# Early copies, weight sums moved to VectorE, and logits steps regrouped in a FFN kernel with LoRA and a two-expert layer

## The chip, the cores and the metric

The kernel runs on one core of one Trainium2 chip. The metric is the device time of one launch in microseconds (us), taken as the median of several runs; a profiled execution gives the trace. TensorE is written PE (PEld for its weight loads), VectorE DVE, ScalarE ACT, GpSimd POOL and SyncE, whose queue issues most DMAs, SP.

## The reference

There are 2048 tokens (8 sequences of 256) of width 1024. First a gated FFN with an adapter chosen for each sequence, then a layer in which each token takes the mean of two of eight experts, added to x:

```python
gate = x @ W_gate.T + (x @ A_gate[i].T) @ B_gate[i].T * 0.5
up   = x @ W_up.T   + (x @ A_up[i].T)   @ B_up[i].T   * 0.5
act  = silu(gate) * up                       # width 2752
y    = act @ W_down.T + (act @ A_down[i].T) @ B_down[i].T * 0.5
logits = y @ Wg + bg                         # 8 experts
top2 = top_k(logits, 2)
out = x + mean_k relu(y @ W_e[k] + b_e[k])   # k in top2
```

All inputs are float32.

## The kernel before

**Arithmetic.** Every fp32 operand is split into a high and a low half in a shorter format: ACT copies it (`w_hi`, `x_hi`, `a_hi`, `d_hi`), then DVE or POOL subtracts (`w_lo`, `x_lo`, `a_lo` on DVE; `d_lo` on POOL). A product is three matmuls (L1637 to L1639). The two large products are done by a seven-product scheme in place of eight: the operands are halves of matrices and their sums (B11, B21, T1 to T4, B22 for x; four sums of weights in the tiles `S_T` to `S_T+3`).

**Stages.** The tokens go in two groups g = 0, 1 of 1024. For each group, TensorE first does 21 pairs q of weight tiles with seven products j each (gate and up), with a half unit after them, then seven stages s of the down product, each of five pieces kp, with a remainder after stages 1, 4, 5 and 6. Piece and remainder together are numbered m = 0 to 38. Sums of weights are made by `mix_w` on POOL; for the first pair of the first group by `mix_w0` on DVE. After a product, `e_copy` (ACT, L1086) and `c_add` (DVE, L1115) take the results out of PSUM, so that the next product of the pair can be accumulated; product j = 3 needs copy k = 0, j = 4 copy 1, j = 5 copy 2 and the last part of j = 6 copy 3. `d_add` (DVE, L1209) takes the stages' results out, and a stage's fourth bank is free only when the first `d_add` of the stage before is done. The adapter of the down product needs `ad_diff`, `ad_hi`, `ad_lo` (L1001, L1007, L1012), which split a block that SP loads at L485; the first matmul of it (L1751) comes after the first piece of a group.

**Logits.** For the first half of a group's tokens DVE computes the logits: 64 calls of `l_step` (L1263) a group, each a multiply and sum over 512 columns with a row of the gate weights. SP loads these rows into two buffers of `ytp` (`load_wb`, L538); the load for row s waits until all four steps of row s - 2 are done. After step 63 come `l_sum` and `choice` (L1244, L1247). TensorE's `early_ranks` (L1898), which is placed behind the third piece of the last stage of g = 1, waits for that choice. For the other half TensorE turns y (`turn2`), ACT copies it (`lt_copy`) and TensorE multiplies (`sum2`, L1890); this is done between the last products of a group and the first ones of the next.

**Order of the work.** Each engine but TensorE has a list of jobs, each added with a key, written by hand in the time of TensorE's operations; the engine executes them in order of the keys, waiting at each for its semaphores:

```python
for _, _, fn, args in sorted(self.jobs, key=lambda j: j[:2]):
    fn(eng, *args)
```

`op(g, n)` is the time of product n (position `pos(q, j)`), `op_m(g, m)` = 228 g + 150 + 2 m that of piece m. A job that waits holds everything behind it on its engine, the DMAs of SP included. The keys around the change:

```python
act.add(key, a_hi, ...);  dve.add(key + 0.2, a_lo, ...)   # key = op_m(g, m) - 3.95
pool.add(op_m(g, m) - 3.5, d_lo, g, m)
sp.add(max(op_m(g, m) - 8.6, ...), load_a, j)             # pieces of the activation
```

Of the kernel before, what the change touches and what calls it, by code (L numbers as in the profile page):

```python
# [10 lines left out]
ALU = mybir.AluOpType  # L11
# [113 lines left out]
def build(nc, xp, xn, wp, agu, bgu, bdn, itok, wgt, wgb, bg, we, be, cst_f, cst_i, ident_d, ut_d, out):  # L125
# [6 lines left out]
    with ctx:  # L132
# [455 lines left out]
        for i in range(i, len(pieces)):  # L588
# [5 lines left out]
            sp.add(keys[i], load, i)  # L594
        for o, key in (("T2", op_m(0, 36) + 1.9), ("T3", op(1, 0) + 1.0), ("T4", op(1, 0) + 3.4)):
            for h in range(2):
                sp.add(key + 0.02 * h, load_x1, o, h)
# [25 lines left out]
        def l_key(g, o):  # L623

            if o < 32:
                return stage_end(g, 1) + 1.5 + 0.88 * o
            return stage_end(g, 4) + (0.3 + 0.45 * (o - 32) if g else 0.6 + 0.6 * (o - 32))

# [121 lines left out]
        for g in range(NG):  # L750
            for q in range(NP):
                if g or q:
                    pool.add(op(g, 0.5 if q == 1 else 7 * q - (6.5 if q else 4.6)), mix_w, g, q)
# [189 lines left out]

        def mix_w0(e, part):

            a = [[w_raw(0, i, j) for j in range(2)] for i in range(2)]
            if part == 0:
                arrived(e, at["w", 0, 0])
                arrived(e, at["w", 0, 1])
                e.tensor_tensor(tile(S_T), a[1][0], a[1][1], ALU.add).then_inc(s_S, 1)  # L950
                e.wait_ge(s_S, 1)
                e.tensor_tensor(tile(S_T + 1), tile(S_T), a[0][0], ALU.subtract).then_inc(s_S, 1)
            else:
                e.wait_ge(s_S, 2)
                e.tensor_tensor(tile(S_T + 2), a[0][1], tile(S_T + 1), ALU.subtract).then_inc(s_S, 1)
                e.tensor_tensor(tile(S_T + 3), a[1][0], a[0][0], ALU.subtract).then_inc(s_S, 1)
# [332 lines left out]
        for g in range(NG):  # L1289
# [12 lines left out]
            for o in XORD:  # L1302
                for h in range(2):
# [5 lines left out]
                    dve.add(key + 0.14, x_lo, g, o, h)  # L1309
            key = op(g, 0) + (0.05 if g else -1.745)  # L1310
            act.add(key, ag_hi, g)
            dve.add(key + 0.01, ag_lo, g)
            key = op(g, 150.95)
            dve.add(key, ad_diff, g)
# [23 lines left out]
            for q in range(NP):  # L1338
                for k in range(4):
                    key = 9.2 if q == 1 and k == 0 else pos(q, [0, 2, 3, 5][k]) + 1.05  # L1340
                    act.add(op(g, key), e_copy, g, q, k)
                    due = op(g, pos(q, [4 if q < 2 else 1, 6, 6, 6][k]) + [1.1, 1.05, 1.1, 1.15][k])
                    dve.add(due, c_add, g, q, k)
                    if q % 2 == 0 and (q < 20 or k < 2):
                        act.add(due + 0.35, silu, g, q, k)
                    if q % 2:
                        dve.add(due + 0.3, gated, g, q, k)
                    elif q == 20 and k >= 2:
                        dve.add(due + 0.3, gated, g, q, k - 2)
# [14 lines left out]
            for o in range(64):  # L1364
                dve.add(l_key(g, o), l_step, g, o)
            dve.add(l_key(g, 63) + 0.01, l_sum, g)
            dve.add(l_key(g, 63) + 0.02, choice, 2 * g)
            for m in range(8):
# [10 lines left out]
        for h in range(2):  # L1379
# [3 lines left out]
            dve.add(2.2 + 0.001 * h, x0_t4, h)  # L1383
        dve.add(-1.5, mix_w0, 0)
        dve.add(0.4, mix_w0, 1)
        for k in range(8):
# [247 lines left out]
        def _(e):  # L1634
# [50 lines left out]
            def product(g, q, j):  # L1685
# [5 lines left out]
                if j == 0:  # L1691
                    if q >= 2:
                        e.wait_ge(s_c, g * 85 + 4 * (q - 1))
                    elif g:
                        e.wait_ge(s_ev, 28 * g)
                    m = main1(g, n, "B11", bk, True, True)
                elif j == 1:
                    m = main1(g, n, "B21", bk + 1, True)
                    if q >= 2:
# [440 lines left out]
```

## Time and profile before

| | |
|---|---|
| median of 3 runs | 1919.98 us (1919.01 to 1924.09) |
| the profiled execution: its own time | 1930.36 us |
| its span, first to last instruction | 1928.2 us |
| mean granted TensorE clock | 0.979 of full speed |
| busy: PE, DVE, ACT, POOL | 96%, 63%, 39%, 56% |

The busy share is that of the whole span. A granted clock of 1.0 is the upper of the two levels (2.4 GHz), 0.5 the lower (1.2 GHz). Times in the trace count from the span's start. An idle time in a timeline row stands in brackets with what ended it.

### The profile page before, as it was taken

The numbers are of one execution on the slowest core, as the hardware profiler recorded it, in microseconds if no ns is written. First come the engines' busy times: TensorE is split into PE (matmuls) and PEld (weight loads), VectorE is DVE, ScalarE is ACT, GpSimd is POOL, SyncE is SP. The second block draws the span as 40 slices with busy tenths as digits, with TensorE's granted clock in tenths as the row PEclk, the third lists the DMA queues.
The fourth block names the chain that finished last, engine by engine and source line by source line (L and its number), as shares of the span: only waits on it lengthen the run. The fifth ranks groups of instructions, "written<-read, shape, count | busy, mean of one in ns | idle before, by whom it ended". The sixth has DMA issues, their size and how long they took to land.

```text
span 1928.2 us, 24887 instructions
## 1 busy us (share of the span) xinstructions
PE 1846.6 (96%) x8679; PEld 1540.2 (80%) x8679; DVE 1208.4 (63%) x1367; ACT 748.7 (39%) x1062; POOL 1084.0 (56%) x647
## 2 busy tenths in 40 slices
PE   4899999999899999999999998999989999999997
PEld 4788888888788878788888887887878888888886
DVE  8688778875458884776677766467886642344300
ACT  4444443443443333444444444343322333333332
POOL 3478888873334452464566643444433766666664
PEclk8999999999999999999999999999998999999998
DMA  5366665645466664344344345466633875677643
GB/s 195 103 219 221 223 222 194 234 154 171 165 228 232 214 197 137 107 130 155 121 150 169 132 140 181 164 232 211 206 116 131 238 190 138 180 188 189 156 90 55
DMA packets 118025, 331.43 MB, mean 172 GB/s; under 512 B 14080, under 2 KB 16000, under 8 KB 117632
## 3 DMA queue, kind: packets, MB, share of 16 engines
q1 hardware_dynamic: 99952, 268.06, 40.8%
q0 software_dynamic: 17952, 61.75, 13.4%
q8 instruction: 77, 1.26, 0.3%
q14 instruction: 44, 0.36, 0.1%
HBM read 248.62 MB, written 90.05 MB: 176 GB/s over the span
## 4 chain that ended last, share of the span: by engine, by line
PE 80%; DVE 7%; DMA 4%; issue 4%; POOL 2%; ACT 2%; SPq 1%; DVEq 0%; ACTq 0%; POOLq 0%
PE PS L1637 24%; PE PS L1638 24%; PE PS L1639 24%; PE PS L1681 2%; DVE FT L1263 2%; PE PS L1751 2%; PE PS L1983 2%; DMA raw<-wt_scratch 2%; DVE R L887 1%; PE PS L1890 1%; PE PS L1668 1%; DVE ring L868 1%; DMA X<-in_xp 1%; DMA FT<-act_scratch 1%; DVE R L918 1%
## 5 line engine op out<-in xcount | busy, mean ns | idle before, releaser
L1637 PE MATMUL PS<-R,ring 128*128 128x512 f32 (+1 forms) x1800 | 711.3, 395 | 41.2 <-issue 31.1
L1638 PE MATMUL PS<-R,ring 128*128 128x512 f32 (+1 forms) x1800 | 705.4, 392 | 0.0
L1639 PE MATMUL PS<-R,ring 128*128 128x512 f32 (+1 forms) x1800 | 704.4, 391 | 0.0
L1637 PEld LDWEIGHTS PS<-R,ring 128*128 128x128 f32 x1800 | 340.8, 189 | 114.3 <-issue 47.6
L1639 PEld LDWEIGHTS PS<-R,ring 128*128 128x128 f32 x1800 | 340.3, 189 | 72.5
L1638 PEld LDWEIGHTS PS<-R,ring 128*128 128x128 f32 x1800 | 340.9, 189 | 66.1
L748 POOL TENSOR_TENSOR ring<-raw,ring 128x1024 fp32r<-128x1024 f32 x78 | 193.2, 2477 | 294.6 <-ACT ring L874 294.5
L1637 PE MATMUL PS<-ring,R 128*128 128x512 f32 x592 | 235.5, 398 | 8.9 <-DVE FT L1209 8.9
L727 POOL DMA_INDIRECT brw<-in_bgu,idx_b x88 | 90.7, 1031 | 269.7 <-DVE R L1032 226.0
L868 DVE TENSOR_TENSOR ring<-FT,ring 128x512 fp32r<-128x512 f32 x168 | 178.6, 1073 | 91.0 <-ACT ring L864 89.3
L1638 PE MATMUL PS<-ring,R 128*128 128x512 f32 x592 | 234.0, 395 | 0.0
L1639 PE MATMUL PS<-ring,R 128*128 128x512 f32 x592 | 233.4, 394 | 0.0
L887 DVE TENSOR_TENSOR R<-FT,R 128x1024 fp32r<-128x1024 f32 x70 | 140.7, 2012 | 98.3 <-ACT R L883 97.9
L864 ACT ACTIVATE ring<-FT 128x512 fp32r<-128x512 f32 x168 | 105.8, 631 | 234.4 <-PE PS L1639 134.0
L1629 DVE CAST R<-raw 128x1024 fp32r<-128x1024 f32 x56 | 67.9, 1212 | 193.0 <-PE PS L1639 170.7
L874 ACT ACTIVATE ring<-raw 128x1024 fp32r<-128x1024 f32 x78 | 82.7, 1060 | 269.7 <-PE PS L1639 150.2
L868 DVE TENSOR_TENSOR ring<-raw,ring 128x512 fp32r<-128x512 f32 x130 | 152.4, 1174 | 53.7 <-ACT ring L864 51.1
L864 ACT ACTIVATE ring<-raw 128x512 fp32r<-128x512 f32 x130 | 81.2, 627 | 153.7 <-PE PS L1639 83.0
L1115 DVE TENSOR_TENSOR FT<-FT,PS 128x512 f32<-128x512 f32 x168 | 110.6, 679 | 47.4 <-PE PS L1681 47.3
L1637 PEld LDWEIGHTS PS<-ring,R 128*128 128x128 f32 x592 | 113.4, 192 | 33.3 <-DVE FT L1209 8.4
L1639 PEld LDWEIGHTS PS<-ring,R 128*128 128x128 f32 x592 | 113.0, 191 | 24.4
L1263 DVE CUSTOM_DVE_ANT_0 FT<-FT,ytp 128x512 f32<-128x512 f32 x128 | 125.5, 1023 | 8.8 <-DMA ytp<-in_wgb 8.7
(189 smaller groups left out, 2356.3 us busy)
## 6 DMA issues: line engine op xcount, KB each, us to landing
raw<-in_wp SPq DMA_DIRECT2D x124, 512.0 KB, 4.2
act_scratch<-FT SPq DMA_DIRECT2D x140, 256.0 KB, 4.8
FT<-act_scratch SPq DMA_DIRECT2D x70, 512.0 KB, 4.8
raw<-in_we SPq DMA_DIRECT2D x64, 512.0 KB, 6.3
raw<-wt_scratch SPq DMA_DIRECT2D x40, 512.0 KB, 6.2
out<-in_xn SPq DMA_DIRECT2D x17, 512.0 KB, 5.1
ytp<-in_wgb SPq DMA_DIRECT2D x32, 256.0 KB, 4.9
y_scratch<-FT SPq DMA_DIRECT2D x7, 1024.0 KB, 7.3
```

What stands on the lines that cost most here:

```text
L727: e.indirect_dma_start(out=brw[0:96, j * 512:(j + 1) * 512], out_offset=None, in_=bgu.rearrange("(r a) n -> r (a n)", a=2), in_offset=ioa( ...
L748: e.tensor_tensor(slot2(n, 1), pair(raw_t(i)), slot2(n, 0), ALU.subtract).then_inc(s_lp, 1)
L864: e.activation(slot(op(g, n), 0), w_src(g, n), ACT.Copy).then_inc(s_hi, 1)
L868: e.tensor_tensor(slot(op(g, n), 1), w_src(g, n), slot(op(g, n), 0), ALU.subtract).then_inc(s_lo, 1)
L874: e.activation(slot2(n, 0), pair(raw_t(i)), ACT.Copy).then_inc(s_hi, 2)
L887: e.tensor_tensor(a_ring(j, 1), raw_a(j), a_ring(j, 0), ALU.subtract).then_inc(s_al, 1)
L1115: e.tensor_tensor(c_tile(q, k), tile(E_T + [0, 2, 0, 1][k]), PS[:, bk + [1, 2, 3, 0][k], :], ALU.add).then_inc(s_c, 1)
L1263: e.tensor_tensor_reduce(out=JK[n % 2], in0=tile(SET_C + tt), in1=ytp[:, (s % 2) * 512:(s % 2) * 512 + 512], scale=1.0, scalar=0.0, op0=AL ...
L1629: link(e.tensor_copy(s_w_t(ex, k, 0), raw_t(i)))
L1637: e.matmul(out_, hi, whi, start=start, stop=False, skip_group_check=True)
L1638: e.matmul(out_, hi, wlo, start=False, stop=False, skip_group_check=True)
L1639: return e.matmul(out_, lo, whi, start=False, stop=stop, skip_group_check=True)
```

## The change

- The copies k = 0, 1, 2 of the first pair of the first group get keys 0.0, 0.25 and 1.25 in place of 1.05, 5.05 and 6.05, so ACT does them before the splits of the operands that come later.
- The four weight sums of the second pair of the first group are made by DVE (`mix_w0` with q = 1, keys 2.5 to 2.52) and no longer by POOL (key 0.5). The first pair's third and fourth sums are parted: keys 0.16 and 1.16 in place of 0.4 for both.
- The 64 logits steps of a group get keys op_m(m) + 2.3, which is 0.05 behind the `a_lo` of piece m + 3: two behind each piece in the first half (m = 10 to 25), then 2, 4, 4, 4, 4, 4, 3, 4, 3 (m = 26 to 34). `l_sum` and `choice` come at op_m(34) + 2.38. Before, the steps lay every 0.88 (first half) and every 0.6 (g = 0) or 0.45 (g = 1). SP's `load_wb` keys follow from the same function.
- The adapter's `ad_diff`, `ad_hi`, `ad_lo` of the down product move from op(g, 150.95) to op(g, 149.0).
- In the first products of g = 1: `ag_hi`, `ag_lo` move from 0.05 to 0.2, behind the split of T2 on ACT; the load of T4 from 3.4 to 2.9; the first product waits for the third `lt_copy` (and the second one for the fourth) in place of all `d_add`s of group 0.

```diff
--- before.py
+++ after.py
@@ -592,7 +592,7 @@
             if e >= 2 and k == 3:
                 sp.add(keys[i], load_bias, e)
             sp.add(keys[i], load, i)
-        for o, key in (("T2", op_m(0, 36) + 1.9), ("T3", op(1, 0) + 1.0), ("T4", op(1, 0) + 3.4)):
+        for o, key in (("T2", op_m(0, 36) + 1.9), ("T3", op(1, 0) + 1.0), ("T4", op(1, 0) + 2.9)):
             for h in range(2):
                 sp.add(key + 0.02 * h, load_x1, o, h)
         for j in range(70):
@@ -623,8 +623,10 @@
         def l_key(g, o):
 
             if o < 32:
-                return stage_end(g, 1) + 1.5 + 0.88 * o
-            return stage_end(g, 4) + (0.3 + 0.45 * (o - 32) if g else 0.6 + 0.6 * (o - 32))
+                m = 10 + o // 2
+            else:
+                m = 26 + sum(o - 32 >= n for n in (2, 6, 10, 14, 18, 22, 25, 29))
+            return op_m(g, m) + 2.3 + 0.001 * o
 
         for g in range(NG):
             for s in range(16):
@@ -749,7 +751,7 @@
 
         for g in range(NG):
             for q in range(NP):
-                if g or q:
+                if g or q >= 2:
                     pool.add(op(g, 0.5 if q == 1 else 7 * q - (6.5 if q else 4.6)), mix_w, g, q)
             for p in range(10):
                 pool.add(op(g, 14 * p) + 16.9, mix_act, g, p)
@@ -941,18 +943,25 @@
             e.wait_ge(s_xl, x_at(0, "B21", h))
             e.tensor_tensor(X0[2][:, hs], X0[2][:, hs], X0[0][:, hs], ALU.subtract).then_inc(s_xp, 1)
 
-        def mix_w0(e, part):
-
-            a = [[w_raw(0, i, j) for j in range(2)] for i in range(2)]
+        def mix_w0(e, q, part):
+
+            a = [[w_raw(0, 2 * q + i, j) for j in range(2)] for i in range(2)]
             if part == 0:
-                arrived(e, at["w", 0, 0])
-                arrived(e, at["w", 0, 1])
+                arrived(e, at["w", 0, 2 * q])
+                arrived(e, at["w", 0, 2 * q + 1])
+                if q:
+                    e.wait_ge(s_lo, lo_of(0, pos(0, 3)))
                 e.tensor_tensor(tile(S_T), a[1][0], a[1][1], ALU.add).then_inc(s_S, 1)
-                e.wait_ge(s_S, 1)
+                e.wait_ge(s_S, 4 * q + 1)
                 e.tensor_tensor(tile(S_T + 1), tile(S_T), a[0][0], ALU.subtract).then_inc(s_S, 1)
-            else:
-                e.wait_ge(s_S, 2)
+            elif part == 1:
+                e.wait_ge(s_S, 4 * q + 2)
+                if q:
+                    e.wait_ge(s_lo, lo_of(0, pos(0, 4)))
                 e.tensor_tensor(tile(S_T + 2), a[0][1], tile(S_T + 1), ALU.subtract).then_inc(s_S, 1)
+            else:
+                if q:
+                    e.wait_ge(s_lo, lo_of(0, pos(0, 5)))
                 e.tensor_tensor(tile(S_T + 3), a[1][0], a[0][0], ALU.subtract).then_inc(s_S, 1)
 
         def e_hi(e, k):
@@ -1307,10 +1316,10 @@
                         key = {"B11": -4.95, "B21": -3.95, "T1": -1.6, "T2": -0.7, "B22": 0.2, "T3": 1.3, "T4": 2.3}[o] + 0.02 * h
                     act.add(key, x_hi, g, o, h)
                     dve.add(key + 0.14, x_lo, g, o, h)
-            key = op(g, 0) + (0.05 if g else -1.745)
+            key = op(g, 0) + (0.2 if g else -1.745)
             act.add(key, ag_hi, g)
             dve.add(key + 0.01, ag_lo, g)
-            key = op(g, 150.95)
+            key = op(g, 149.0)
             dve.add(key, ad_diff, g)
             act.add(key + 0.01, ad_hi, g)
             dve.add(key + 0.02, ad_lo, g)
@@ -1338,6 +1347,8 @@
             for q in range(NP):
                 for k in range(4):
                     key = 9.2 if q == 1 and k == 0 else pos(q, [0, 2, 3, 5][k]) + 1.05
+                    if g == 0 and q == 0 and k < 3:
+                        key = [0.0, 0.25, 1.25][k]
                     act.add(op(g, key), e_copy, g, q, k)
                     due = op(g, pos(q, [4 if q < 2 else 1, 6, 6, 6][k]) + [1.1, 1.05, 1.1, 1.15][k])
                     dve.add(due, c_add, g, q, k)
@@ -1363,8 +1374,8 @@
                     dve.add(key, d_add, g, s, i)
             for o in range(64):
                 dve.add(l_key(g, o), l_step, g, o)
-            dve.add(l_key(g, 63) + 0.01, l_sum, g)
-            dve.add(l_key(g, 63) + 0.02, choice, 2 * g)
+            dve.add(op_m(g, 34) + 2.38, l_sum, g)
+            dve.add(op_m(g, 34) + 2.39, choice, 2 * g)
             for m in range(8):
                 key = [-1.5, -1.3, -1.0, -0.7, 0.3, 0.4, 0.5, 0.6][m] if g else [-1.5, -1.3, -1.0, -0.7, 1.0, 1.1, 2.0, 2.1][m]
                 act.add(stage_end(g, 6) + key, lt_copy, g, m)
@@ -1381,8 +1392,9 @@
             dve.add(-0.8 + 0.001 * h, x0_t2, h)
             dve.add(1.2 + 0.001 * h, x0_t3, h)
             dve.add(2.2 + 0.001 * h, x0_t4, h)
-        dve.add(-1.5, mix_w0, 0)
-        dve.add(0.4, mix_w0, 1)
+        for q in range(2):
+            for part in range(3):
+                dve.add([[-1.5, 0.16, 1.16], [2.5, 2.51, 2.52]][q][part], mix_w0, q, part)
         for k in range(8):
             act.add(keys[at["e", 0, k]], e_hi, k)
             dve.add(keys[at["e", 0, k]] + 0.1, e_lo, k)
@@ -1692,9 +1704,14 @@
                     if q >= 2:
                         e.wait_ge(s_c, g * 85 + 4 * (q - 1))
                     elif g:
-                        e.wait_ge(s_ev, 28 * g)
+                        if q:
+                            e.wait_ge(s_ev, 28 * g)
+                        else:
+                            e.wait_ge(s_lc, 8 * g - 5)
                     m = main1(g, n, "B11", bk, True, True)
                 elif j == 1:
+                    if g and q == 0:
+                        e.wait_ge(s_lc, 8 * g - 4)
                     m = main1(g, n, "B21", bk + 1, True)
                     if q >= 2:
                         m = lora1_out(g, q, 0, 0, bk + 1)
```

## Rows read from the trace of the kernel before

**Rows 1.** The first line of the page.

```profile
span 1928.2 us, 24887 instructions
```

**Rows 2.** Waits of TensorE (line, releaser: us in total, times, longest).

```profile
PE PS L1751 <- DVE R L1012: 11.7, 2, 5.8
...
PE PS L1898 <- DVE msk L1247: 3.9, 1, 3.9
```

**Rows 3.** Timeline of TensorE where it resumes: start, us, operation, [idle before <-releaser].

```profile
54.57 0.76 PE L1637 MATMUL PS<-R,ring 128*128 128x512 f32 x1 [16.28 <-issue]
...
493.59 1.22 PE L1751 MATMUL PS<-R 128*128 128x256 f32 x4 [5.84 <-DVE R L1012]
...
722.05 0.47 PE L1637 MATMUL PS<-ring,R 128*128 128x512 f32 x1 [2.12 <-DVE FT L1209]
...
737.00 0.77 PE L1637 MATMUL PS<-R,ring 128*128 128x512 f32 x1 [3.27 <-issue]
...
771.81 0.47 PE L1637 MATMUL PS<-R,ring 128*128 128x512 f32 x1 [1.36 <-issue]
...
777.38 0.47 PE L1637 MATMUL PS<-R,ring 128*128 128x512 f32 x1 [2.36 <-issue]
```

**Rows 4.** Windows: us, busy by engine, then PEclk, DMA share, GB/s.

```profile
493.50:498.50 5.00, 4.91 (x17) 4.24 (x18) 0.72 (x2) 2.00 (x2) 1.58 (x1) 0.55 0.00 0
722.00:727.00 5.00, 4.95 (x19) 4.13 (x20) 2.90 (x5) 0.60 (x1) 0.44 (x1) 0.66 0.62 223
...
1205.40:1211.90 6.50, 6.48 (x20) 5.52 (x21) 2.24 (x1) 2.00 (x2) 2.37 (x1) 0.54 0.01 3
```

**Rows 5.** Timeline of ScalarE, start-up.

```profile
53.87 0.60 ACT L1086 ACTIVATE FT<-PS 128x512 f32<-128x512 f32 x1
```

**Rows 6.** Timeline of VectorE, start-up.

```profile
29.51 2.35 DVE L918 TENSOR_TENSOR R<-FT,R 128x1024 fp32r<-128x1024 f32 x2
...
37.70 5.15 DVE L936 TENSOR_TENSOR X<-X,FT 128x1024 f32<-128x1024 f32 x2
42.78 3.43 DVE L918 TENSOR_TENSOR R<-X,R 128x1024 fp32r<-128x1024 f32 x2
...
52.42 0.68 DVE L868 TENSOR_TENSOR ring<-raw,ring 128x512 fp32r<-128x512 f32 x1
...
71.10 1.29 DVE L1115 TENSOR_TENSOR FT<-FT,PS 128x512 f32<-128x512 f32 x2 [0.56 <-PE PS L1681]
```

**Rows 7.** Timeline of GpSimd, start-up.

```profile
39.70 2.07 POOL L665 TENSOR_TENSOR FT<-FT,raw 128x512 f32<-128x512 f32 x1
```

**Rows 8.** Source view of the load of the adapter block, L485.

```profile
L485 SPq DMA_DIRECT2D FT<-ad_scratch x2: 319/319/319, 470.7 to 1183.5; - x2
...
DMA to landing us min/median/max: 3.9/3.9/4.0
```

**Rows 9.** Timeline of VectorE before the first stage.

```profile
478.12 2.48 DVE L1173 TENSOR_TENSOR R<-FT,R 128x512 fp32r<-128x512 f32 x1 [0.78 <-ACT R L1165]
...
490.58 0.56 DVE L1001 TENSOR_TENSOR FT<-FT 128x160 f32<-128x160 f32 x2
491.70 1.83 DVE L1012 TENSOR_TENSOR R<-FT,R 128x352 fp32r<-128x352 f32 x4 [0.56 <-ACT R L1007]
```

**Rows 10.** Source view of the logits step, L1263.

```profile
L1263 DVE CUSTOM_DVE_ANT_0 FT<-FT,ytp x128: 676/681/3226, 568.8 to 1428.9; 128x512 f32<-128x512 f32 x128
```

**Rows 11.** Source view of the low halves of the activation pieces, L887.

```profile
L887 DVE TENSOR_TENSOR R<-FT,R x70: 1211/2570/3420, 469.0 to 1433.2; 128x1024 fp32r<-128x1024 f32 x70
```

**Rows 12.** Timeline of VectorE, last stage of the second group.

```profile
1412.97 3.23 DVE L1263 CUSTOM_DVE_ANT_0 FT<-FT,ytp 128x512 f32<-128x512 f32 x1
...
1431.17 1.90 DVE L1244 TENSOR_TENSOR oh<-cf,mi 128x64 bf16<-128x64 f32 x1
```

**Rows 13.** Timeline of GpSimd, same stretch.

```profile
1413.23 2.41 POOL L748 TENSOR_TENSOR ring<-raw,ring 128x1024 fp32r<-128x1024 f32 x1
```

**Rows 14.** Timeline of ScalarE, fifth stage of the second group.

```profile
1335.26 1.06 ACT L874 ACTIVATE ring<-raw 128x1024 fp32r<-128x1024 f32 x1 [9.57 <-DMA raw<-in_wp]
```

More of the change, by code:

```diff
@@ L942, in x0_t4 @@
             e.tensor_tensor(X0[2][:, hs], X0[2][:, hs], X0[0][:, hs], ALU.subtract).then_inc(s_xp, 1)
-        def mix_w0(e, part):
-            a = [[w_raw(0, i, j) for j in range(2)] for i in range(2)]
+        def mix_w0(e, q, part):
+            a = [[w_raw(0, 2 * q + i, j) for j in range(2)] for i in range(2)]
             if part == 0:
-                arrived(e, at["w", 0, 0])
-                arrived(e, at["w", 0, 1])
+                arrived(e, at["w", 0, 2 * q])
+                arrived(e, at["w", 0, 2 * q + 1])
+                if q:
+                    e.wait_ge(s_lo, lo_of(0, pos(0, 3)))
                 e.tensor_tensor(tile(S_T), a[1][0], a[1][1], ALU.add).then_inc(s_S, 1)
-                e.wait_ge(s_S, 1)
+                e.wait_ge(s_S, 4 * q + 1)
                 e.tensor_tensor(tile(S_T + 1), tile(S_T), a[0][0], ALU.subtract).then_inc(s_S, 1)
-            else:
-                e.wait_ge(s_S, 2)
-                e.tensor_tensor(tile(S_T + 2), a[0][1], tile(S_T + 1), ALU.subtract).then_inc(s_S, 1)
+            elif part == 1:
+                e.wait_ge(s_S, 4 * q + 2)
+                if q:
+                    e.wait_ge(s_lo, lo_of(0, pos(0, 4)))
+                e.tensor_tensor(tile(S_T + 2), a[0][1], tile(S_T + 1), ALU.subtract).then_inc(s_S, 1)
+            else:
+                if q:
+                    e.wait_ge(s_lo, lo_of(0, pos(0, 5)))
                 e.tensor_tensor(tile(S_T + 3), a[1][0], a[0][0], ALU.subtract).then_inc(s_S, 1)
```

## The prediction

> **What bounds the kernel now.** The page first: a span of 1928.2 us [rows 1] of which TensorE is busy 96% (the table above), so what can be won is TensorE's idle time and its slow time. I read the waits of TensorE next, then its timeline at each idle place, and then, at each place, the queue of the engine that ended the wait. The waits view [rows 2] shows two waits of 5.84 us for the adapter's low halves (one a group) and one of 3.94 us for the first choice of the second group. The timeline [rows 3] shows the rest that the change touches: 16.28 us at 54.57 in the start-up, 2.12 us at the end of group 0, then 3.27, 1.36 and 2.36 us in the first products of group 1. After such an idle time TensorE also runs at the lower clock level: in the windows view [rows 4] the granted clock is 0.55 and 0.54 (near the 1.2 GHz level) after the two waits of 5.84 us, which loses 4.9 x 0.45 = 2.2 and 6.5 x 0.46 = 3.0 us, and 0.66 after the 2.12 us, which loses 1.7 us; the stretches after 737.00 and 777.38 look the same, 1.7 us each. After 1.36 us alone nothing is lost. All engines but TensorE have idle time, so an edit counts only by the wait that it ends. All terms are against the profiled execution (1928.2 us span, 1930.4 us with what lies around it); the runs shown have a median of 1919.98 us, 0.5% less, so I take the same microseconds off that.
>
> **Start-up.** TensorE resumes at 54.57 because product j = 4 waits for copy 1, which ACT executes at 53.87 [rows 3, 5]. The copy's source was complete at about 29 us (TensorE's timeline); it stood behind the splits of T3, T4 and of five weight tiles. With the new keys copies 0 and 1 run at about 28 and 31 us, and j = 4 is bound by the split of its weights on DVE. From here on DVE's queue sets the pace, so I count its work up to the split for j = 6, which ends at 53.1 [rows 6].
> - Removed: the sums of T3 and T4 and the low halves of T3 take 5.15, 3.43 and, at 46.73, 3.43 us again for two instructions of 128x1024 each, where such a pair takes 2.35 us undisturbed [rows 6]; GpSimd's weight sums run beside them (2.07 us each, [rows 7]). With those gone from POOL: -2.80 - 1.08 - 1.08 = -5.0 us.
> - Removed: about 1.1 us in which DVE waited for ACT at 33 us.
> - Added: four weight sums of 128x512 on DVE, each the size of the split at 52.42, 0.68 us less 0.07 of overlap: +2.5 us. They precede the split for j = 6 and delay it.
> - So that split ends near 49.5. Behind it are nine short instructions (two of the adapter's, three splits, one addition, two low halves of the adapter product, in all 5 us), which the adapter's part of j = 6 needs: 54.5, then copy 3 and four small matmuls: 55.2. In the trace the additions that follow j = 6 start at 71.10 [rows 6]. The difference is 15.8 us; I take 15.0, as a low-clock stretch may remain after the two shorter idle times (near 3.5 and 2 us). Bounds: 10 (copies help, the sums fill the rest) and 16.5.
> GpSimd's sums for the third pair start at once on the load that waits for the split of j = 6, so they move along.
>
> A rule of the Trainium skill speaks against the second half of this: Perfetto Trace Analysis, section Optimizing Scalar/DVE Operations, says that GpSimd and VectorE share a read port, so that moving work between them might not help. With it alone, the start-up would give about 12.5 in place of 15.0; the pairs of 5.15 against 2.35 us in [rows 6] rather show that the sum on DVE costs less than what it disturbs from POOL.
>
> **The adapter of the down product.** SP issues the block's load at 470.7 and it lands after 4.0 us [rows 8], at 474.7. DVE executes `ad_diff` at 490.58, last of its list before the stage, and `ad_lo` at 491.70, ended 493.5 [rows 9]. With the key 149.0 it comes behind the split at 478.12, which ends at 480.6: 0.56 + 0.56 of waiting for ACT + 1.83 = 483.6. TensorE needs it at 487.75, so the wait goes, with 4 us to spare. What is late instead: ACT holds the third piece's copies 1.5 to 3.5 us, `a_lo(2)` ends near 485.3 and POOL's low half near 487.4, needed at 495; the half unit's chain ends 2 us later, needed after 510. No wait arises. Both groups: 2 x 5.84 + 2.2 + 3.0 = 16.9 us. Bounds: 12 (the clock falls anyway) and 17.
>
> **Group 1's first products.** The first product writes bank 0; the third `lt_copy` has already been waited for by the matmul before it, so 3.27 us go. T4's load moves ahead of two weight loads of which the first waits for POOL; ACT reaches T4 early and copies 1 and 2, which stood behind it, follow their products: 1.36 + 2.36 us go. With the clock: 7.0 + 2 x 1.7 = 10.4 us. What could rise is `s_L` 5, needed by the second adapter product, with a margin of some 1.4 us. Bounds: 5 and 10.5.
>
> **Logits steps.** A step takes 0.68 us, 3.2 at most [rows 10], when GpSimd works beside it; 128 steps remain 128 steps. A piece's `a_lo` takes 1.21 to 3.42 us in the same way [rows 11].
> - End of group 0: five steps stood behind the last `a_lo`, now three. 2 x 0.61 us earlier, and the choice then runs before GpSimd's sums begin (1.8 us less); `d_add` of the last stage, now at 721.2, comes near 718.5, before TensorE's 719.93. -2.12 - 1.7 = -3.8 us. But in the fifth stage four steps, not three, precede the `d_add` of group 0, and the fourth meets GpSimd's next piece, as in group 1 at 1412.97 [rows 12, 13], where TensorE idled 0.9 us: +1.0 us. Net -2.8.
> - End of group 1: the choice that `early_ranks` waits for ends at 1433.3 [rows 12]. Before the last `a_lo` there were 63 steps, after the change 61; but the last `a_lo` and three steps come before the choice, and 54 to 58 are behind the `d_add` of stage 5. From there DVE has no idle time: five steps more (5 x 0.61) and one `a_lo` more (1.14 undisturbed): +4.2 us on a wait of 3.94, and a longer low clock as after 5.84 us, +0.9: +5.1 us. Bounds: +1 (GpSimd meets fewer of them) and +8.
> - First halves: steps 8 and 9, 18 and 19 still stand before the `d_add`s, so the waits there (1.21, 1.76, 2.89 us) stay. SP's `load_wb` waits for a step that comes 0.6 to 2.9 us later at two places: +1.0 us. Bounds: -2 and +5.
>
> Here one rule can be weighed. The trace has a step that starts at 1412.97, 0.26 us before GpSimd's instruction, and still takes 3.23 us [rows 12, 13]. The Trainium skill, SBUF — State Buffer, section Who interferes with whom, has it that whoever is first holds the shared pair of ports for the whole instruction and the other is blocked. By it the fourth step would take 0.68 us and the +1.0 would be 0; the row decides, and I keep it.
>
> **The sum.** -15.0 - 16.9 - 10.4 - 2.8 + 5.1 + 1.0 = -39.0 us. The profiled span would be 1889 us, the median 1919.98 - 39 = 1881 us. Behind the stages, in the expert blocks, nothing is changed, and TensorE is busy there, so all of it passes to the end.
>
> **Rivals.**
> - *The adapter's wait is taken up next* (13%): with TensorE 8 us ahead, the pieces' loads are late. For it: loads were issued during the 5.84 us. Against: the next three pieces' weights had landed by 490. It would give back half of 16.9: 1889.5 us.
> - *The load queue* (17%): in the first halves, `load_wb` stands directly in front of the activation and weight loads and waits for the two steps before it. For it: before 1335.26 ACT waited 9.57 us for a weight load [rows 14] that SP issued late behind such a `load_wb`, and TensorE then idled 2.89 us and lost 3.1 us by the clock, 6.0 in all. Two more such places: 1881 + 12 = 1893 us.
> - *Slower* (3%): the same queue at many places. It decides from seven more such places on (7 x 6.0 = 42 > 39); at eight, 1929 us. Against: SP waits for the same splits now as before, only 1 to 3 us longer.
> - *The change does not do what it says in the start-up* (5%): the sums on DVE cost what they free; 12.5 in place of 15.0: 1883.5 us. This is what the sharing rule above would give.
> - My forecast, 1881 us: 62%.
>
> **How the numbers follow.** The likeliest case with its own bounds reaches from 1872 to 1890; the queue's case with one more place goes to 1899, and I leave its tail and the slower case out: 1871 to 1899. A measurement of this kernel tells about 0.3% (6 us) from no change. Faster by more than that: 62 + 13 + 17 + 5 = 97%, less 2 for a queue case that eats nearly all: 95%. Same 2%, slower 3%.
>
> **What would show it.** Right: TensorE idle between 28 and 56 us is about 8 us, not 21; DVE's sums of T3 and T4 take 1.2 us each; no idle at the first L1751 of either group and a clock of 1.0 there; no idle at the first product of group 1; `early_ranks` waits about 8 us. Wrong: L1637 idle behind DMAs of SP in the second to fourth stage, more than 6 us in sum than before; `early_ranks` waiting 4 us or less (then I overrated the regrouping's cost, and the time is near 1876); or a new wait of the second adapter product for `s_L`.

## The result, and the profile after

The changed kernel takes 1906.02 us (median of 5 runs, 1903.87 to 1909.91), the kernel before, timed beside it, 1921.42 us (1919.01 to 1925.28). The ratio is 0.9923, 95% interval 0.9903 to 0.9942: 0.8% faster, 15 us. I had forecast 1881 us and a range of 1871 to 1899, so the direction was right and the size was not: less than half of the 39 us came. The profiled executions differ by 24.0 us (1904.2 against 1928.2 us span); 9 us more than the medians, since the one profiled execution of before was 9 us above its median. That part is looked at with the first experiment, e0.

The waits of TensorE in the changed kernel (line, releaser: us in total, times, longest):

```profile
PE PS L1649 <- DVE FT L1218: 17.3, 6, 6.6
PE PS L1649 <- DVE R L920: 9.4, 1, 9.4
PE PS L1915 <- DVE msk L1256: 8.7, 1, 8.7
PE PS L1649 <- DVE ring L870: 6.5, 3, 3.8
PE PS L1768 <- DVE R L889: 5.8, 2, 3.5
```

The 11.7 us of [rows 2] for the adapter's low halves are gone. `early_ranks` (now L1915) waits 8.7 us in place of 3.9. The first line had 8.9 us, 5 times, 2.9 at most before: TensorE now waits 17.3 us for `d_add` (L1218). The last line is new: TensorE waits for a piece's `a_lo` (L889). The timeline of TensorE shows the places:

```profile
34.60 0.50 PE L1649 MATMUL PS<-R,ring 128*128 128x512 f32 x1 [1.90 <-DVE ring L870]
49.86 0.50 PE L1649 MATMUL PS<-R,ring 128*128 128x512 f32 x1 [3.81 <-DVE ring L870]
55.34 1.02 PE L1693 MATMUL PS<-R 96*128 96x256 f32 x6 [1.02 <-DVE R L1063]
...
594.71 0.98 PE L1768 MATMUL PS<-R 128*128 128x256 f32 x6 [2.33 <-DVE R L889]
...
612.03 0.80 PE L1649 MATMUL PS<-ring,R 128*128 128x512 f32 x1 [6.55 <-DVE FT L1218]
...
712.53 0.47 PE L1649 MATMUL PS<-ring,R 128*128 128x512 f32 x1 [2.24 <-DVE FT L1218]
...
1302.58 1.21 PE L1768 MATMUL PS<-R 128*128 128x256 f32 x8 [3.47 <-DVE R L889]
...
1320.75 0.79 PE L1649 MATMUL PS<-ring,R 128*128 128x512 f32 x1 [5.79 <-DVE FT L1218]
...
1415.78 0.19 PE L1915 MATMUL PS<-msk,ut 128*128 128x12 bf16 x1 [8.70 <-DVE msk L1256]
```

The start-up (54.57 in [rows 3] is now 34.60) and the first products of group 1 (no idle time left there) went as forecast. The waits at 594 and 1302 stand at the last piece of stage s = 3, those at 612 and 1320 at the first piece of s = 4 (stages counted from 0), all in the first half of the logits steps. The windows view gives the clock beside them (columns as in [rows 4]):

```profile
474.00:479.00 5.00, 5.00 (x27) 4.31 (x26) 2.24 (x4) 3.98 (x6) 0.43 (x1) 1.00 0.34 108
...
612.00:620.00 8.00, 7.97 (x23) 6.38 (x24) 6.29 (x9) 3.06 (x3) 5.43 (x3) 0.64 0.81 269
```

At the adapter (474) the clock is now 1.00, where [rows 4] had 0.55; after the 6.55 us wait it is 0.64 for 8 us, 2.9 us lost.

**The same points of the program in both traces (milestones).** Both traces have 8679 matmul records in the same order, so the end of the same one is taken in both. The table gives what each stretch added to the changed kernel's lead, in us; a stretch is closed where TensorE is back at the full clock in both.

| stretch | forecast | profiled |
|---|---|---|
| start-up | -15.0 | -13.7 |
| adapter, both groups | -16.9 | -8.1 - 8.8 |
| first products of group 1 | -10.4 | -10.9 |
| first halves of the steps | +1.0 | +11.0 + 6.9 |
| end of group 0 | -2.8 | +1.3 |
| end of group 1 (`early_ranks` and the low clock after it) | +5.1 | +5.0 |
| what follows in group 1 (TensorE turning y, first experts) to the last product | 0 | -6.7 |

(The texts of e1 and e3 below carry a first reading with other bounds: 10.7 and 8.1 for the first halves, 1.9 for the end of group 0.) The first three terms hold within 1.3 us each. One term is off by 17 us, and it decided the outcome. For it, read what SyncE's queue does in stage s = 3 of group 0 (L538 is `load_wb`, L429 `load_a`, L412 and L416 loads of weights or of an operand):

```profile
582.30 0.33 SPq L538 DMA_DIRECT2D ytp<-in_wgb  x1
582.67 0.43 SPq L429 DMA_DIRECT2D FT<-act_scratch  x1
583.20 0.38 SPq L416 DMA_DIRECT2D raw<-wt_scratch  x1
583.62 0.43 SPq L416 DMA_DIRECT2D raw<-in_xp  x1
584.57 0.32 SPq L429 DMA_DIRECT2D FT<-act_scratch  x1
584.93 0.67 SPq L412 DMA_DIRECT2D raw<-in_wp  x1
598.11 0.33 SPq L538 DMA_DIRECT2D ytp<-in_wgb  x1
```

Six DMAs leave within 3.3 us, then none for 12.5 us, until the next `load_wb` goes. What happens in between, on ScalarE and then on VectorE:

```profile
590.07 1.06 ACT L876 ACTIVATE ring<-raw 128x1024 fp32r<-128x1024 f32 x1 [10.05 <-DMA raw<-wt_scratch]
591.03 1.04 ACT L885 ACTIVATE R<-FT 128x1024 fp32r<-128x1024 f32 x1
```

```profile
592.10 2.56 DVE L889 TENSOR_TENSOR R<-FT,R 128x1024 fp32r<-128x1024 f32 x1 [6.34 <-ACT R L885]
594.58 0.68 DVE L1272 CUSTOM_DVE_ANT_0 FT<-FT,ytp 128x512 f32<-128x512 f32 x1
...
595.19 2.88 DVE L1272 CUSTOM_DVE_ANT_0 FT<-FT,ytp 128x512 f32<-128x512 f32 x1
```

It is a closed loop through SyncE's queue, a load, ScalarE and VectorE. The weight tile issued at 583.20 lands at 590.0, ScalarE splits it (`d_hi`) and then the activation piece, `a_lo` follows, then the two steps 14 and 15, and at 598.07 the next `load_wb`, which waits for step 15, lets the next weight tile go. One turn takes 15.8 us (550.62, 566.40, 582.30, 598.11 are the issues of `load_wb`) and brings two pieces. TensorE needs 12.8 us for two. So each turn takes 3.0 us from the lead that the split pieces have over TensorE, and when the lead is used up TensorE waits: 2.33 + 6.55 us.

### The profile page after: what moved, and what is told of

It is laid out like the page before. It is cut to its first block, busy times and chain, and to the rows that moved or that the text cites. A ratio compares the mean times of both kernels' runs of the same rounds, so it can differ in the third digit from the quotient of the medians.

```text
span 1904.2 us, 24886 instructions
## 1 busy us (share of the span) xinstructions
PE 1835.0 (96%) x8679; PEld 1529.2 (80%) x8679; DVE 1205.3 (63%) x1371; ACT 748.5 (39%) x1062; POOL 1082.8 (57%) x643
## 4 chain that ended last, share of the span: by engine, by line
PE 72%; POOL 8%; DVE 8%; issue 5%; DMA 5%; ACT 1%; SPq 1%; POOLq 0%; ACTq 0%; DVEq 0%
PE PS L1649 22%; PE PS L1650 21%; PE PS L1651 21%; DVE R L889 2%; DVE FT L1272 2%; DMA raw<-wt_scratch 2%; PE PS L1693 2%; PE PS L2000 2%; PE PS L1768 2%; DMA raw<-in_wp 1%; POOL brw L729 1%; POOL FT L672 1%; POOL FT L667 1%; POOL FT L664 1%; PE PS L1907 1%
## 5 line engine op out<-in xcount | busy, mean ns | idle before, releaser
L1649 PE MATMUL PS<-ring,R 128*128 128x512 f32 x592 | 235.7, 398 | 17.7 <-DVE FT L1218 17.3
L889 DVE TENSOR_TENSOR R<-FT,R 128x1024 fp32r<-128x1024 f32 x70 | 148.4, 2122 | 117.8 <-ACT R L885 117.5
L1649 PEld LDWEIGHTS PS<-ring,R 128*128 128x128 f32 x592 | 113.4, 192 | 43.3 <-DVE FT L1218 17.6
L1651 PEld LDWEIGHTS PS<-ring,R 128*128 128x128 f32 x592 | 113.1, 191 | 24.3
L1650 PEld LDWEIGHTS PS<-ring,R 128*128 128x128 f32 x592 | 113.2, 191 | 22.0
```

The source lines that it names most:

```text
L889: e.tensor_tensor(a_ring(j, 1), raw_a(j), a_ring(j, 0), ALU.subtract).then_inc(s_al, 1)
L1649: e.matmul(out_, hi, whi, start=start, stop=False, skip_group_check=True)
L1650: e.matmul(out_, hi, wlo, start=False, stop=False, skip_group_check=True)
L1651: return e.matmul(out_, lo, whi, start=False, stop=stop, skip_group_check=True)
```

## The experiments

One thousandth of the time is 1.9 us; every ratio is to the kernel before, timed on the same chip, with its 95% interval.

**e0: the kernel before, a second profile.**

> The kernel before, once more, unchanged, for a second profile of it. The first profiled execution was 9 us above the median of its runs (1930.4 against 1921.4). If that was its clock alone, this one shows the same idle places (16.3 us at 54.6, 5.8 us twice, 3.3 and 2.4 us) and fewer low-clock stretches, above all in the one of 13.65 us near 1457 and of 12.66 us at the end. If the idle places differ, the waits themselves vary from run to run.

It took 1923.95 us (span 1921.9), with the same idle places within 0.5 us each, but for the 1.36 us at 771.81 [rows 3], which is 0.32 us in it. Of the 6 us between the two profiles nearly all lies behind 1300, and 2.4 us in one stretch almost without waits, the turns behind the last stage. The windows view over that stretch, first the first profile, then this one:

```profile
1434.00:1470.00 36.00, 36.00 (x206) 32.15 (x204) 14.79 (x57) 5.97 (x10) 1.91 (x2) 0.78 0.47 161
```

```profile
1432.00:1468.00 36.00, 35.75 (x213) 31.22 (x212) 16.99 (x66) 5.86 (x10) 1.91 (x2) 0.85 0.45 161
```

Nearly the same work, another granted clock (0.78 and 0.85 over 36 us: 2.5 us). Taken against this second profile, the last line of the table above is -2.0 in place of -6.7 us: most of it is not the change. None of my terms lay there. The changed kernel's profile is 17.7 us shorter than this one, near the 15 us of the medians.

**e1: the changed kernel with the steps where they were.**

```diff
-                m = 10 + o // 2
-            else:
-                m = 26 + sum(o - 32 >= n for n in (2, 6, 10, 14, 18, 22, 25, 29))
-            return op_m(g, m) + 2.3 + 0.001 * o
+                return stage_end(g, 1) + 1.5 + 0.88 * o
+            return stage_end(g, 4) + (0.3 + 0.45 * (o - 32) if g else 0.6 + 0.6 * (o - 32))
...
-            dve.add(op_m(g, 34) + 2.38, l_sum, g)
-            dve.add(op_m(g, 34) + 2.39, choice, 2 * g)
+            dve.add(l_key(g, 63) + 0.01, l_sum, g)
+            dve.add(l_key(g, 63) + 0.02, choice, 2 * g)
```

> The changed kernel with the logits steps, their sum and choice and with them the loads of the weight rows at the keys of before; all else as changed. Theory (the regrouping of the first halves starves TensorE: its milestones lost 10.7 us in group 0 and 8.1 us in group 1 where I had put 1.0 for both): these and the 4.8 us at early_ranks and 1.9 us at the end of group 0 come back, 1906 - 25 = 1881 us, ratio to before 0.979. Rival (the first halves would have lost it anyway, since TensorE arrives there 22 us earlier and the loads are late): only the 6.7 us at the ends come back, 1899 us, ratio 0.988.

1880.44 us, ratio 0.9791 (0.9767 to 0.9816). The theory's 1881 came; the rival's 0.988 is outside the interval. So the regrouping costs 25 us in the changed kernel, and the other three parts together bring 40 us where my sum has 42.3. In stages s = 3 and 4 its profile has waits of 1.58, 1.42 and 2.81 us, nearly those of before, where the changed kernel has the 2.3, 6.6, 3.5 and 5.8 us.

**e2: the same steps, the row loads behind the piece loads.**

```diff
-                sp.add(l_key(g, 4 * max(s - 2, 0) + 3) - (4 if s < 2 else 0) + 0.02, load_wb, g, s)
+                sp.add(l_key(g, 4 * max(s - 2, 0) + 3) - (4 if s < 2 else 0) + (1.92 if 2 <= s < 10 else 0.02), load_wb, g, s)
```

> The changed kernel with one thing moved: the loads of weight rows 2 to 9 of each group come 1.9 later on the SP queue, behind the weight and activation loads of the next pieces instead of in front of them; the steps themselves stay. Theory (a loop: the row's load waits for two steps, the piece loads stand behind it, the splits wait for them, the steps stand behind the splits; 15.8 us for two pieces, of which the two steps are 3.5 us, where TensorE needs 13.3 us): the waits of 2.3 and 6.6 us in group 0 and 3.5 and 5.8 us in group 1 go, 1906 - 18 = 1888 us, ratio 0.983. Rival (the steps directly behind a split hold up VectorE itself, whatever the queue does): no change, 1906 us, ratio 0.992.

1883.81 us, ratio 0.9799 (0.9780 to 0.9817), 22 us under the changed kernel where the theory had 18; the rival's 0.992 is out. All four waits are gone with one number on SyncE's queue, with the order of the steps on VectorE untouched. The same stretch of that queue and of ScalarE:

```profile
585.35 2.37 SPq L412 DMA_DIRECT2D raw<-in_wp  x2
587.77 0.47 SPq L538 DMA_DIRECT2D ytp<-in_wgb  x1
591.40 0.34 SPq L429 DMA_DIRECT2D FT<-act_scratch  x1
591.78 0.43 SPq L412 DMA_DIRECT2D raw<-in_wp  x1
597.81 0.33 SPq L429 DMA_DIRECT2D FT<-act_scratch  x1
```

```profile
580.33 1.06 ACT L876 ACTIVATE ring<-raw 128x1024 fp32r<-128x1024 f32 x1 [4.41 <-PE PS L1768]
...
586.75 1.06 ACT L876 ACTIVATE ring<-raw 128x1024 fp32r<-128x1024 f32 x1 [3.46 <-PE PS L1768]
...
593.17 1.06 ACT L876 ACTIVATE ring<-raw 128x1024 fp32r<-128x1024 f32 x1 [4.41 <-PE PS L1768]
```

The loads now leave every 6.4 us, one piece at a time, and ScalarE waits for TensorE to free a buffer, no longer for a DMA. That is the sign that the order is right: the splits follow TensorE every 6.42 us (12.8 for two pieces), and the load side has time to spare. The three waits of before in these stages (1.21, 1.76, 2.89 us), which I had taken as staying, are gone too.

**e3: the regrouping alone in the kernel before.** The reverse of e1's diff, on the kernel before.

> The kernel before with the regrouped steps alone (keys of steps, sum, choice and row loads). Theory: its cost adds up as in the changed kernel, 10.7 + 8.1 + 1.9 + 4.8 = 25 us slower: 1946 us, ratio 1.013. Rival (the regrouping costs only because TensorE arrives early there): 6 us at early_ranks and 1 us elsewhere, 1928 us, ratio 1.003. My prediction had +3.3 us for it.

1950.66 us, ratio 1.0151 (1.0130 to 1.0173): 29 us slower, a little more than the theory's 25; the rival is out. TensorE waits 2.28, 4.86, 3.70 and 6.01 us at the same places, and between 573 and 620 `load_wb` goes every 15.5 to 15.9 us. The loop does not need TensorE to arrive early. In group 0:

```profile
616.93 1.21 PE L1753 MATMUL PS<-R 128*128 128x256 f32 x8 [2.28 <-DVE R L889]
634.13 0.80 PE L1639 MATMUL PS<-ring,R 128*128 128x512 f32 x1 [4.86 <-DVE FT L1211]
```

**e4: e2 and the second halves as before.** e2's diff, and from e1's diff the second `return` and the keys of `l_sum` and `choice`.

> The changed kernel with the row loads 2 to 9 behind the piece loads (as in e2) and the steps of the second halves, the sum and the choice at the keys of before (as in e1); the first halves keep two steps behind each piece. Theory (early_ranks waits 8.7 us because one split and the regrouped steps come before the choice): it waits under 1 us as in e1 and the low-clock stretch of 10.2 us after it goes to 3.4 us, while the first addition of the last stage costs 2.1 in place of 0.8 us: e2's 1883.8 - 5.5 = 1878 us, ratio 0.9775. Rival (the low clock or another wait takes it): 1884 us as e2, ratio 0.980.

1879.76 us, ratio 0.9765 (0.9739 to 0.9792). The time is the theory's, though e4's interval overlaps that of e2, so the times alone do not show the step. The milestones do: the end of group 1 costs 0.1 us against before, in e2 5.4. The theory's picture is not quite right: `early_ranks` waits as long as it did before the change.

```profile
1381.93 0.19 PE L1914 MATMUL PS<-msk,ut 128*128 128x12 bf16 x1 [3.94 <-DVE msk L1255]
```

In e1, with the same order of VectorE's queue there, it waits 0.85 us:

```profile
1389.40 0.19 PE L1913 MATMUL PS<-msk,ut 128*128 128x12 bf16 x1 [0.85 <-DVE msk L1254]
```

Over the profiles with the old second half this is one of two patterns: 0.9 us at the last stage's `d_add` and 3.94 here (before, e0, e4, e8, e9), or 2.12 to 2.14 and at most 0.85 (e1, e5, e6, e7). The profiles have one thing that goes with it: in the four of the second pattern VectorE waits 2.1 to 2.5 us for a row of gate weights some 30 us before `early_ranks`, and in none of the first pattern does it. In e1:

```profile
1358.69 1.10 DVE L1270 CUSTOM_DVE_ANT_0 FT<-FT,ytp 128x512 f32<-128x512 f32 x1 [2.09 <-DMA ytp<-in_wgb]
```

Why that row comes late in those four was not isolated by an experiment.

**e5 to e8: one part each, on the kernel before.** The edits are the parts of the change's own diff: the three copies; `mix_w0` with its keys and `mix_w`'s `q >= 2`; the key 149.0; the hunks of group 1.

> The kernel before with the three early copies alone. From my prediction's sum: the copies free j = 3 and j = 4, and then VectorE's splits, slowed by GpSimd's sums as before (5.15 and 3.43 us pairs), set the split for j = 6 near 52: 11 to 12.5 us, 1909.5 us, ratio 0.994. Rival (the early copies hold up ScalarE's splits of T2 to T4 by 0.6 us each and VectorE waits for them): 8 us, 1913.5 us, ratio 0.996.

> The kernel before with the weight sums of the second pair on VectorE alone (the first pair's third and fourth sums parted with them). Theory (copy 1 on ScalarE at 53.9 stays what j = 4 waits for, and what ScalarE does before it waits for VectorE's splits, which come 2.5 us earlier): 2.5 us faster, 1919 us, ratio 0.9987. Rival (the Trainium skill, Perfetto Trace Analysis, Optimizing Scalar/DVE Operations: the shared port makes the move worth nothing): 0, ratio 1.000. The profile tells them apart: the sums of T3 and T4 take 2.35 us a pair or 5.15 and 3.43.

> The kernel before with the three splits of the down product's adapter at key 149.0 alone. From my prediction's sum: both waits of 5.84 us and both low-clock stretches of 6.83 us go: 16.9 us faster, 1904.6 us, ratio 0.991; in the changed kernel's trace the milestones gained 8.0 and 8.5 us there. Rival (without the earlier start the piece loads or the first additions take part of it back): 8 us, ratio 0.996.

> The kernel before with the edits of group 1's first products alone (the third and fourth lt_copy waited for in place of all d_adds, ag_hi and ag_lo behind the split of T2, the load of T4 0.5 earlier). From my prediction's sum: the waits of 3.27, 1.36 and 2.36 us and two low-clock stretches go: 10.4 us faster, 1911 us, ratio 0.9946; in the changed kernel's trace the milestones gained 11.2 us there. Rival (the second adapter product waits for s_L, or the load of T4 only moves the wait to the weight loads): 5 us, ratio 0.9974.

| part alone | forecast of its term | measured, us | ratio, interval |
|---|---|---|---|
| e5 copies | -12.5 | -11.1 | 0.9942 (0.9921 to 0.9964) |
| e6 sums on VectorE | -2.5 | -6.1 | 0.9968 (0.9951 to 0.9985) |
| e7 adapter keys | -16.9 | -15.2 | 0.9921 (0.9897 to 0.9945) |
| e8 group 1's first products | -10.4 | -7.5 | 0.9961 (0.9943 to 0.9979) |

Their sum is -39.9 us, e1 measured -40.2: the parts add up, within intervals of 3 to 5 us to either side of each. e6 is clear of zero; its theory (0.9987) lies just outside on the other side. The Trainium skill (Perfetto Trace Analysis, Optimizing Scalar/DVE Operations) says that moving work between GpSimd and VectorE might not help, as they share a read port; the rival took that as worth nothing, and fell. The trace of e6 shows the pairs of [rows 6] (5.15 and 3.43 us) with no sum of GpSimd beside them:

```profile
36.47 2.36 DVE L936 TENSOR_TENSOR X<-X,FT 128x1024 f32<-128x1024 f32 x2
38.82 2.36 DVE L918 TENSOR_TENSOR R<-X,R 128x1024 fp32r<-128x1024 f32 x2
```

TensorE resumes at 49.12 instead of 54.57. What GpSimd no longer does is worth more than what VectorE does in its place (four instructions of 0.68 us). By the milestones the gain there is 4.3 us, inside the interval. The interval of e7 leaves out its rival (0.996). Those of e5 and e8 hold both theory and rival; by the milestones e5's start-up gains 10.0 us, and e8, with none of the three waits in its profile, 10.9 us.

**e9 to e11: what was left over.** e9 changes e4:

```diff
-                dve.add(key + 0.13, w_lo, g, n)
+                dve.add(2.49 if (g, n) == (0, 8) else op_m(0, 38) + 0.085 if g and n < 2 else key + 0.13, w_lo, g, n)
...
-                key = op(g, [2.1, 5.2][w] if g else [1.17, 7.1][w])
+                key = op(g, [2.1, 5.2][w] if g else [1.17, 3.6][w])
```

> The mended kernel (e4) with two reorderings on VectorE. In the start-up the split of the weights for j = 6 comes before the four weight sums, and the adapter product's halves (t1_hi, t1_lo for the second part) right behind the sums instead of behind three splits. At the end of group 0 the splits of group 1's first two weight tiles come behind the first additions of the last stage (L1217) instead of in front. Theory: TensorE's 3.8 us before j = 6 goes to 1.2, its adapter part follows about 2.5 us earlier; the 2.25 us wait at 700 goes, since the first addition stood 2.4 us behind those splits: 1879.8 - 4.7 = 1875 us, ratio 0.974. Rival (the 2.25 us is set by the steps and the choice before the splits; GpSimd's third pair meets the sums in the start-up): no change, 1880 us, ratio 0.9765.

1877.77 us, ratio 0.9775 (0.9749 to 0.9801), not to be told from e4; the theory's 0.974 is outside. One half did what it should: the 2.25 us wait at the end of group 0 is gone from TensorE's timeline, so it did hang on the two splits in front of `d_add`. The other half moved its wait on:

```profile
52.48 0.47 PE L1692 MATMUL PS<-R 96*128 96x256 f32 x2 [2.46 <-DVE R L1062]
56.83 1.22 PE L1692 MATMUL PS<-R 96*128 96x256 f32 x4 [3.88 <-ACT FT L1094]
```

TensorE starts j = 6 at 46.99 instead of 49.77, then waits for copy 3 on ScalarE, which waits for an addition that I had left behind three splits. By the milestones the start-up ends 3.3 us later than in e4. e10 moves `early_ranks` behind the fourth piece of the last stage:

```diff
-                        if g == NG - 1 and s == 6 and kp == 2:
+                        if g == NG - 1 and s == 6 and kp == 3:
                             early_ranks()
```

> As e9, with early_ranks behind the fourth piece of the last stage instead of the third. Theory: the 3.9 us wait for the choice and the 3.4 us of low clock after it (1.7 us lost) go: e9 - 5.6 us, 1869.5 us, ratio 0.971. Rival (the ranks of the first half come 3 us later, and the table on GpSimd that waits for them becomes late behind the last piece): up to 3 us given back, 1872.5 us, ratio 0.9727.

1871.90 us, ratio 0.9744 (0.9717 to 0.9771). The wait of 3.9 us goes, 0.84 us appears at the table behind the last piece, and the wait for the one on GpSimd grows from 0.5 to 1.25 us, as the rival had it in part. e11 brings the addition and copy 3 forward:

```diff
-                    if g == 0 and q == 0 and k < 3:
-                        key = [0.0, 0.25, 1.25][k]
+                    if g == 0 and q == 0:
+                        key = [0.0, 0.25, 1.25, 7.44][k]
...
-                    dve.add(due, c_add, g, q, k)
+                    dve.add(3.62 if (g, q, k) == (0, 0, 0) else due, c_add, g, q, k)
```

> As e10, with the wait that e9 opened closed: in e9 and e10 TensorE, done with j = 6 of the first pair at 50.0, waited 2.5 us for the adapter's halves and then 3.9 us for copy 3 on ScalarE, which stood behind silu and a weight split, which in turn waited for the addition at 54.3 on VectorE. Here that addition (key 3.62) comes before the next three weight splits and copy 3 (key 7.44) before silu. Theory: copy 3 ends near 53.7 instead of 57.0, TensorE resumes 3.3 us earlier and the low clock after it is 3.4 us instead of 6.8: 1872 - 4 = 1868 us, ratio 0.972. Rival (the three splits behind the addition are then what product j = 2 of the second pair waits for, or the 2.5 us are followed by another late half): 1872 us as e10, ratio 0.974. Both kernels of the study are beaten if it stays under 1880.

1869.62 us, ratio 0.9723 (0.9703 to 0.9743), which holds the theory's 0.972 and the rival's 0.974. In its timeline the wait for copy 3 is down to

```profile
53.80 1.23 PE L1692 MATMUL PS<-R 96*128 96x256 f32 x4 [0.84 <-ACT FT L1094]
```

With that the start-up is where it was in e4: e9's half of it and e11 together gain nothing. This is the fastest version measured: 2.8% under the kernel before and, by the two ratios, 2.0% under the changed one. The steps from e4 on (0.9765, 0.9775, 0.9744, 0.9723) are each within one another's intervals or next to it; e11 against e4 is 0.4%, intervals just overlapping, and the spans of their profiled executions are equal (1871.0 and 1870.9 us; that of e4 was the fastest of its six). So only single waits are shown to go, and that e11 is faster than e4 is likely but not shown.

## Why the prediction was wrong, step by step

- **What bounds the kernel**: right. Every term sat at an idle place of TensorE, and the parts add up.
- **Start-up, -15.0**: right. -13.7 in the profiles, and the idle time between 28 and 56 us is 7.5 us where I had written about 8; e5 and e6 give 11.1 and 6.1 us. The case that the sums on VectorE cost what they free (12.5 in all) fell with e6, which pays by itself; of my own split, -12.5 and -2.5, the sums had too little rather than too much.
- **Adapter, -16.9**: right, -17.0 in the profiles, -15.2 alone. No load became late behind it; that rival fell.
- **Group 1's first products, -10.4**: right in the profiles (-10.9); -7.5 alone, with an interval up to 11.
- **End of group 1, +5.1**: right, +5.0 in the profiles. The wait is 8.70 us, 4.8 more; from e2 to e4, where the second halves go back to the old keys, this stretch gives 5.3 us back (the ratio falls by 0.0034, 6.5 us, with intervals that overlap).
- **End of group 0, -2.8**: wrong, +1.3. The +1.0 came (0.83 us at 686.88). The 2.12 us did not go (2.24 us). The step that failed is "`d_add` of the last stage, now at 721.2, comes near 718.5, before TensorE's 719.93": it still comes 1.4 us behind the point where TensorE is ready, 1.3 before. The two steps put in front of the last `a_lo` only changed what meets GpSimd's `d_lo`: before, a step (2.87 us) with `a_lo` already done in 1.21, now `a_lo` itself (3.40 us). The two weight splits in front of `d_add` take 2.35 us as before, the second one beside GpSimd's sums (1.75 in place of 0.68 us). I had held the collisions where they were. e9 shows the two splits as what to move.
- **First halves, +1.0**: this is the step that made the prediction wrong. I wrote that "SP's `load_wb` waits for a step that comes 0.6 to 2.9 us later at two places", as a delay that is paid once. It is paid in every turn of the loop, and a loop longer than TensorE's pace has no place to recover. The waits that were to stay did not have to either: with the loop open (e2) they are gone. The profiles have +11.0 and +6.9 us in place of +1.0. One turn of it: `load_wb`, directly in front of `load_a`; 0.9 us later the weight load, which lands after 6.8 us; `d_hi`, `a_hi` 2 us; `a_lo` 2.6; two steps 0.68 and, with GpSimd beside, 2.9: 15.8 us against 12.8. I costed the single wait of SyncE and never walked the turn. e2 opens the loop and gets 22 us back, e3 closes it in the kernel before and loses 29.
- **The rival on the load queue** named this mechanism, 17%, but priced it at two places, 12 us; it was worth 17.9 us. The waits in the first halves are 19.2 us (2.33 + 6.55 + 1.05 + 3.47 + 5.79) against 5.9 before, and the low clock adds the rest. The slower rival was the same queue at eight places; in e3, where nothing was won beside it, it did end slower.

What stays open: what makes the row of gate weights late in one of the two patterns at the end of group 1, and how much of e3's 29 us over e1's 25 is chance.

## What to carry to other kernels

When a DMA that waits for compute is put in front of other loads on one queue, follow the loads round until the path comes back to the DMA; if it does, add up one turn and set it against the pace of the bounding engine for the same work, and not the delay of one instance. A load that is needed late goes behind the loads that are needed soon, even if its own condition is met earlier. Where a wait is taken away, read what stands behind it in each of the queues: e9 shows how one that is left out takes the gain.

## What the runs showed of the hardware

- When a logits step and a GpSimd subtraction overlap, the one that starts first nearly always keeps its time and the other one waits. In the trace before, 22 steps start 0.00 to 0.61 us ahead of GpSimd's instruction and take 0.68 or 0.69 us; GpSimd's takes up to 2.94 us in place of 2.40. In 20 pairs GpSimd's is first, and there the step takes up to 2.92 us and ends 0.55 us after it. One of the 22:

```profile
1419.66 0.68 DVE L1263 CUSTOM_DVE_ANT_0 FT<-FT,ytp 128x512 f32<-128x512 f32 x1
```

```profile
1419.78 2.83 POOL L748 TENSOR_TENSOR ring<-raw,ring 128x1024 fp32r<-128x1024 f32 x1 [4.14 <-ACT ring L874]
```

- There is one exception, that of [rows 12, 13]: the step starts 0.26 us ahead, takes 3.23 us, four times what it takes alone, and GpSimd's instruction keeps its 2.41. In the changed kernel it comes at two places, 682.98 and 1390.64:

```profile
1390.64 3.24 DVE L1272 CUSTOM_DVE_ANT_0 FT<-FT,ytp 128x512 f32<-128x512 f32 x1
```

```profile
1389.97 0.92 POOL L738 DMA_INDIRECT brw<-in_bdn,idx_d  x1 [0.30 <-issue]
1390.90 2.42 POOL L750 TENSOR_TENSOR ring<-raw,ring 128x1024 fp32r<-128x1024 f32 x1
```

The Trainium skill, SBUF — State Buffer, section Who interferes with whom, has the one that is first block the other: over the 14 profiles 254 of the steps that start ahead go by it and 16 do not. In all 16 GpSimd comes straight from issuing an indirect DMA (0.01 to 0.02 us before), in none of the 254. Why that turns the order round is not shown. The +1.0 us that I took from the row, against the rule, came at such a place.

- The granted clock differs between executions of one kernel over a stretch with nearly the same work (0.78 and 0.85 over 36 us); two profiles of the same code differ by 6 us in span. A profile's span isn't a median: terms read from waits hold, the difference of two spans doesn't.
- In a burst each load lands later after its issue than the one ahead of it: of the six at 582.30 to 584.93 the five of 512 KB took 6.0, 6.8, 7.7, 8.0 and 8.9 us. The last is one of `raw<-in_wp`, whose median over all 124 is 4.2 us; the second, from `wt_scratch`, is near its median of 6.6 us.
